# Attention kernel on one core: the high and low parts of the queries are made where they leave PSUM

## What is computed

```python
# layer 0, per token: router over 8 LoRA experts; a_sum = sum of four lora_A products
w = softmax(x @ router_W.T + router_b)
h = nan_to_num(x + SCALING * sum_n w[n] * (a_sum @ lora_B[n].T))       # (4, 512, 1024)
# layer 1: cross attention of 512 tokens on 64 context tokens, 32 heads of 32, then layer norm
Q = (h @ Wq.T + bq); K = (ctx @ Wk.T + bk); V = (ctx @ Wv.T + bv)
attn = softmax(where(mask, Q.K / sqrt(32), -inf))
z = h + (attn @ V) @ Wo.T + bo
out = (z - mean(z)) / sqrt(var(z) + 1e-5) * ln_g + ln_b
```

## Time and profile before

| | |
|---|---|
| median of 3 runs | 742.64 us |
| lowest and highest | 741.37 and 742.81 us |
| span of the profiled execution, first to last instruction | 742.5 us |
| PE busy | 692.8 us (93%) |
| DVE busy | 507.3 us (68%) |
| ACT busy | 322.9 us (43%) |
| POOL busy | 307.7 us (41%) |
| the 16 DMA engines busy | 30.9% |

### The profile page before, as it was taken

How to read it: one execution, slowest core, us unless ns; L and a number is a source line. 1 busy time by engine, 2 the same in 40 slices (tenths; PEclk the granted TensorE clock), 3 DMA queues, 4 the chain that set the end, 5 groups by cost and what they waited for, 6 DMA issues and landing times.

```text
span 742.5 us, 14399 instructions
## 1 busy us (share of the span) xinstructions
PE 692.8 (93%) x4736; PEld 635.2 (86%) x4736; DVE 507.3 (68%) x1169; ACT 322.9 (43%) x1061; POOL 307.7 (41%) x343
## 2 busy tenths in 40 slices
PE   4999999999999999999978869999998999999993
PEld 4896599999999999999978768878887887888883
DVE  1458247465564747364666898999899898998733
ACT  0313211222112212212126997778776778777511
POOL 0111012121121121111233775478767786787644
PEclk9999999999999999999998989999999999999998
DMA  9984121713031311211131363013312232222311
GB/s 284 344 309 163 63 90 38 238 44 128 15 129 41 113 57 54 101 42 71 42 113 58 117 202 95 16 46 123 110 50 86 86 116 85 85 85 72 114 57 57
DMA packets 57012, 76.83 MB, mean 103 GB/s; under 512 B 17025, under 2 KB 38657, under 8 KB 56961
## 3 DMA queue, kind: packets, MB, share of 16 engines
q1 hardware_dynamic: 56960, 76.21, 30.7%
HBM read 48.94 MB, written 27.26 MB: 103 GB/s over the span
## 4 chain that ended last, share of the span: by engine, by line
PE 68%; DVE 17%; issue 6%; ACT 5%; DMA 2%; SPq 1%; POOL 0%; DVEq 0%; ACTq 0%
PE ps L501 18%; PE ps L503 17%; PE ps L502 17%; PE ps L586 4%; PE ps L512 4%; PE ps L599 4%; DVE s_sb L834 2%; DVE p_lo L851 2%; DVE kbd_lo L812 2%; PE ps L531 2%; DVE s_sum L844 1%; PE ps L628 1%; DVE vbd_lo L821 1%; ACT s_sb L1021 1%; DVE act_lo L856 1%
## 5 line engine op out<-in xcount | busy, mean ns | idle before, releaser
L501 PE MATMUL ps<-act_hi,w_hi 128*128 128x256 f32 x512 | 149.1, 291 | 0.6 <-issue 0.6
L503 PE MATMUL ps<-act_hi,w_lo 128*128 128x256 f32 x512 | 145.5, 284 | 0.0
L502 PE MATMUL ps<-act_lo,w_hi 128*128 128x256 f32 x512 | 145.5, 284 | 0.0
L1098 POOL TENSOR_TENSOR h_t<-pos,neg 128x256 f32<-128x256 f32 x64 | 48.2, 753 | 234.1 <-DVE neg L743 234.1
L501 PE MATMUL ps<-w_hi,act_hi 128*128 128x512 f32 x256 | 105.5, 412 | 4.1 <-DVE act_lo L856 4.1
L947 ACT ACTIVATE act_hi<-h_t 128x256 fp32r<-128x256 f32 x64 | 26.7, 418 | 179.5 <-DVE h_t L750 179.5
L503 PE MATMUL ps<-w_hi,act_lo 128*128 128x512 f32 x256 | 100.1, 391 | 0.0
L1021 ACT ACTIVATE s_sb<-s_sb,s_min 128x64 f32<-128x64 f32 x256 | 85.7, 338 | 32.7 <-DVE s_min L839 32.1
L502 PE MATMUL ps<-w_lo,act_hi 128*128 128x512 f32 x256 | 100.0, 390 | 0.0
L501 PEld LDWEIGHTS ps<-act_hi,w_hi 128*128 128x128 f32 x512 | 98.8, 193 | 0.8 <-issue 0.8
L502 PEld LDWEIGHTS ps<-act_lo,w_hi 128*128 128x128 f32 x512 | 98.9, 193 | 0.0
(11 more groups left out here) (102 smaller groups left out, 1721.8 us busy)
## 6 DMA issues: line engine op xcount, KB each, us to landing
x_sb<-xT SPq DMA_DIRECT2D x8, 1024.0 KB, 5.7
h_rows<-hn_sb SPq DMA_DIRECT2D x32, 256.0 KB, 2.2
q_cols<-q_sb SPq DMA_DIRECT2D x32, 256.0 KB, 2.0
q_raw<-q_cols SPq DMA_DIRECT2D x32, 256.0 KB, 3.2
z_sb<-h_rows SPq DMA_DIRECT2D x16, 512.0 KB, 3.7
out<-z_sb SPq DMA_DIRECT2D x16, 512.0 KB, 2.9
wk_raw<-WkT SPq DMA_DIRECT2D x8, 512.0 KB, 7.9
wv_raw<-WvT SPq DMA_DIRECT2D x2, 2048.0 KB, 10.9
```

Of the source, the lines that this page charges most:

```text
L501: pe.matmul(dst, lh, rh, start=(first and j == 0), stop=False)
L502: pe.matmul(dst, lh, rl, start=False, stop=False)
L503: mm = pe.matmul(dst, ll, rh, start=False, stop=(last and j == n - 1))
L1098: pool.tensor_tensor(h_t[m % 4][:], pos[m % 2][:], neg[m % 2][:], ALU.add).then_inc(sign_ready, 1)
```

## The change

ScalarE's `copy_q` now writes the rounded high part to q_sb, and VectorE gets a new `q_low`, which forms the low part from the same PSUM tile, the bias and the high part (one scalar_tensor_tensor). q_copied, on which TensorE waits before it writes that PSUM tile again and SP before it stores, is now signalled by `q_low`; qhi_done comes from `copy_q`. Both parts go to DRAM and back (512 KB a transfer for two chunks), straight into tiles that `scores` reads. `q_high` on ScalarE and the old `q_low` on GpSimd are gone, with q_raw, q_hi and q_lo. `scores` waits for the load itself; `load_q` waits for s_mm, the scores of m-3, as that is what frees its tile. In phase A `q_low` stands in VectorE's program wherever UNIT_A has a "q"; in the first eight steps of phase B it stands behind VectorE's step. The larger q_sb takes 4 KB more of a partition; for it a scratch area that the DMA software keeps in SBUF is made smaller.

```diff
 REGION_3 = max(2 * KC * U + 2 * RC * U + 6 * U + 2 * U // 4, 4 * TU * HPC * V + 8 * U + 8 * U + 4 * U + 2 * KC * V)
-REGION_4 = max(4 * U + 2 * NR * R + KC * LOG + 8 * P * TU + H + NR + TU * (R + 2 * NR + 3) + 64, 2 * H)
+REGION_4 = max(4 * U + 2 * NR * R + KC * LOG + 12 * P * TU + H + NR + TU * (R + 2 * NR + 3) + 64, 2 * H)
...
     hn_d = nc.dram_tensor("h_rows", (NB, UB, U, H), F32, kind="Internal").ap()
-    q_d = nc.dram_tensor("q_cols", (NB, UB, KC // 2, P, 2 * U), F32, kind="Internal").ap()
+    q_d = nc.dram_tensor("q_cols", (NB, UB, KC // 2, P, 4 * U), F32, kind="Internal").ap()
...
         p_lo = [sb(f"p_lo{k}", [P, 2, U], F32R, region3) for k in range(2)]
-        q_hi = [sb(f"q_hi{k}", [P, U], F32R, region3) for k in range(4)]
-        q_lo = [sb(f"q_lo{k}", [P, U], F32R, region3) for k in range(4)]
-        q_raw = [sb(f"q_raw{k}", [P, 2, U], F32, region3) for k in range(2)]
+        q_in_sb = [sb(f"q_in_sb{k}", [P, 2, 2, U], F32R, region3) for k in range(2)]
         k_b = sb("k_b", [P, KC, V], F32, region3)
...
         hn_sb = [sb(f"hn_sb{k}", [P, TU, 2 * P], F32, region4) for k in range(2)]
-        q_sb = [sb(f"q_sb{k}", [P, 2, U], F32, region4) for k in range(2)]
+        q_sb = [sb(f"q_sb{k}", [P, 2, 2, U], F32R, region4) for k in range(2)]
         bo_b = sb("bo_b", [P, H], F32, region4)
...
         hn_stored = [sem(f"hn_stored{k}") for k in range(2)]
-        q_mm, q_copied = sem("q_mm"), sem("q_copied")
+        q_mm, qhi_done, q_copied = sem("q_mm"), sem("qhi_done"), sem("q_copied")
         q_stored = [sem(f"q_stored{k}") for k in range(2)]
...
         q_in = [sem(f"q_in{k}") for k in range(2)]
-        qhi_done, qlo_done = sem("qhi_done"), sem("qlo_done")
         s_mm, s_scaled, min_done = sem("s_mm"), sem("s_scaled"), sem("min_done")
...
                 dst = q_d[i, p, g] if p >= 0 else q_d[i - 1, UB - 1, g]
-                sp.dma_start(dst, q_sb[g % 2][:].rearrange("p a n -> p (a n)")).then_inc(q_stored[g % 2], 16)
+                sp.dma_start(dst, q_sb[g % 2][:].bitcast(F32).rearrange("p l a n -> p (l a n)")).then_inc(q_stored[g % 2], 16)
...
                 p, g = m // KC, (m % KC) // 2
-                wait(sp, qlo_done, i * CB + m - 2)
-                sp.dma_start(q_raw[g % 2][:].rearrange("p a n -> p (a n)"), q_d[i, p, g]).then_inc(q_in[g % 2], 16)
+                wait(sp, s_mm, i * CB + m - 2)
+                sp.dma_start(q_in_sb[g % 2][:].bitcast(F32).rearrange("p l a n -> p (l a n)"), q_d[i, p, g]).then_inc(q_in[g % 2], 16)
...
                 c = m % KC
-                wait(pe, qlo_done, i * CB + m + 1)
+                q_both = q_in_sb[c // 2 % 2]
+                wait(pe, q_in[c // 2 % 2], i * 64 + 16 * (m // 4 + 1))
                 wait(pe, klo_done, 8 * i + 8 * (m // CB) + (8 if c >= 4 else 4))
...
                     mm = three(ps_s[c % 2][:, t * 256:(t + 1) * 256],
-                               [(q_hi[c % 4][:, rows], q_lo[c % 4][:, rows], kbd_hi[:, c, :], kbd_lo[:, c, :])])
+                               [(q_both[:, 0, c % 2, rows], q_both[:, 1, c % 2, rows], kbd_hi[:, c, :], kbd_lo[:, c, :])])
                 mm.then_inc(s_mm, 1)
...
+            def q_low(i, m):
+                c = m % KC
+                wait(dve, qhi_done, i * CB + m + 1)
+                dve.scalar_tensor_tensor(q_sb[c // 2 % 2][:, 1, c % 2, :], ps_q[c % 2], bq_c[:, c:c + 1],
+                                         q_sb[c // 2 % 2][:, 0, c % 2, :], ALU.add, ALU.subtract).then_inc(q_copied, 1)
+
             def update(i, m):
...
             dve.wait_ge(router_in, 32)
-            run_phase_a(dve, {"project": copy_values, "route": router, "expand": u_low, "update": update, "query": lambda i, m: None,
+            run_phase_a(dve, {"project": copy_values, "route": router, "expand": u_low, "update": update, "query": q_low,
                               "flush": flush, "rows": last_h_rows})
...
-            run_phase_b(dve, step, lambda m: None)
+            run_phase_b(dve, step, lambda m: q_low(NB - 1, KC * (UB - 1) + m))
...
                 wait(act, q_stored[c // 2 % 2], i * 64 + 32 * (m // KC) + 16 * (c // 4))
-                act.activation(q_sb[c // 2 % 2][:, c % 2, :], ps_q[c % 2], ACT.Identity, bias=bq_c[:, c:c + 1]).then_inc(q_copied, 1)
+                act.activation(q_sb[c // 2 % 2][:, 0, c % 2, :], ps_q[c % 2], ACT.Identity, bias=bq_c[:, c:c + 1]).then_inc(qhi_done, 1)
...
-            def q_high(i, m):
-                g = m % KC // 2
-                wait(act, q_in[g % 2], i * 64 + 16 * (m // 4 + 1))
-                wait(act, s_mm, i * CB + m - 3)
-                act.activation(q_hi[m % 4][:], q_raw[g % 2][:, m % 2, :], ACT.Copy).then_inc(qhi_done, 1)
-
             def exponential(i, m):
...
                         (k_high if place == "k" else v_high)(i, half)
-                if live(i, m, CB):
-                    q_high(i, m)
                 if live(i, m - 7, CB):
...
-            def q_low(i, m):
-                wait(pool, qhi_done, i * CB + m + 1)
-                pool.tensor_tensor(q_lo[m % 4][:], q_raw[m % KC // 2 % 2][:, m % 2, :], q_hi[m % 4][:],
-                                   ALU.subtract).then_inc(qlo_done, 1)
-
             def normalise_p(i, m):
...
                 p, c = m // KC, m % KC
-                if live(i, m, CB):
-                    q_low(i, m)
                 if live(i, m - 2, CB):
...
     }
-    nc = bacc.Bacc("TRN2", target_bir_lowering=False, num_devices=1)
+    nc = bacc.Bacc("TRN2", target_bir_lowering=False, num_devices=1, dynamic_dma_scratch_size=1024)
     args = [nc.dram_tensor(n, a.shape, mybir.dt.from_np(a.dtype), kind="ExternalInput").ap() for n, a in arrays.items()]
```

## The result

The changed kernel takes 750.67 us in the median of four runs (749.99 to 751.91), the kernel before 742.03 us beside it (741.37 to 742.81): a ratio of 1.0114, 95% interval 1.0095 to 1.0133. The forecast was 745.2 us, with a range up to 749.5. The direction was right, the size was not.

What follows compares the result with a forecast made beforehand. TensorE was taken to bound phase A, TensorE and VectorE in turns phase B. Row copies +4.1, boundary +1.5, opening +1.0, relief -4.0 made +2.6 us on a 742.5 us span: 745.1, stated as 745.2, range 739.8 to 749.5.

Steps and rivals of the forecast that it cites:

- as a load it costs nothing. What counts is the order: Phase A: 64 moved low parts, 22 us of VectorE time, fit its idle time; only what stands behind them matters.
- The row copies, +4.1: Phase A: q_low(0) ahead of the row copies delays TensorE 0.62 us in six units, 0.4 in the seventh; +4.1 us.
- The boundary, +1.5: Between phases A and B: first scores 1.5 us later, from 0.4 delay plus 2.0 larger transfers less 0.9 relief.
- relief of kbd_lo: Boundary: GpSimd's q_low no longer runs beside the four kbd_lo, which take 2.59 us; 0.9 us back.
- The landing of k_b: Boundary: larger query loads and store ahead of k_b hold it up by 1.6 to 2.5 us, taken as 2.0.
- I count no change: Boundary: TensorE's slow clock behind the pause is there before and after, so no cost.
- The opening of phase B, +1.0: First eight steps of phase B: q_low(m) behind ScalarE's copy_q(m) delays VectorE; +1.0 us, between 0 and 2.5.
- The relief, -4.0: Three later batches: without GpSimd's q_low, k and v splits stretch less, 0.4 us in ten splits; -4.0 us.
- Loads hidden: Phase B: doubled loads and stores stay hidden; the next batch's k_b keeps about 4 us of slack.
- The first: Rival, faster: phase B gets down to TensorE's pace, removing all 9.2 us, giving 740.0 us; chance 0.17.
- second: Rival, no change: boundary and opening steps of phase B cost nothing, giving 742.7 us; chance 0.17.
- The third: Rival, much slower: k_b late in three batches, giving 749 us; chance 0.15, including dearer boundary and opening.

Runs made afterwards that it cites:

- a_spread219: Changed kernel with 219 more VectorE instructions, spread over three idle stretches: 744.08 us, ratio 1.0036 to the kernel before.
- e1_rows_first: Changed kernel with VectorE's low part of q0 put behind the three row copies in each unit of phase A: 747.33 us, ratio 1.0067.
- second profile of before: Profile of another run of the unchanged kernel before: span 739.1 us at a time of 740.91 us.
- b_kv_late: Kernel before, with k_b and v_b loads of batches 1 to 3 issued only after scores(13) of the batch before: 743.29 us, ratio 1.0016.
- run 14: Kernel before with 37 more VectorE instructions at its start and k_b and v_b loads released by the scaling of group 13: 747.53 us, one run.
- a_pad256: Changed kernel with 256 more VectorE instructions ahead of the loop, which keeps its place in a 256-instruction block: 760.47 us, ratio 1.0246.
- b_pad37: Kernel before with 37 more VectorE instructions at its start, so the loop stands where the changed kernel has it: 743.89 us, ratio 1.0038.
- a_pad219: Changed kernel with 219 more VectorE instructions, so the loop has the kernel before's place in a 256-instruction block: 749.88 us, ratio 1.0108.
- run 7: Changed kernel with only the high part going through DRAM, 256 KB a transfer, same waits and issue order: 746.35 us, ratio 1.0056.
- b_pad37_kv_later: Same run as run 14: kernel before, 37 more VectorE instructions, k_b and v_b loads released by the scaling of group 13: 747.53 us.
- best_unrolled: Changed kernel with row copies first, k_b and v_b ahead of query loads in every batch, phase B's loop written out: 733.38 us, ratio 0.9878.
- run 12: Same run as a_spread219: changed kernel with 219 more VectorE instructions spread over idle stretches: 744.08 us, ratio 1.0036.
- b_again: Kernel before, unchanged, run and profiled once more: 742.33 us, ratio 0.9998.

## Why the prediction was wrong

**The step that failed** is the sentence on the moved low parts, "as a load it costs nothing. What counts is the order". I counted 64 instructions as VectorE's time and looked for what stands behind each; I didn't count them as length of VectorE's program. They move the loop of phase B by 37 instructions, and in that place VectorE stands still for 5.34 us when it jumps back. Priced by a_spread219 this is 6.6 us of 8.6 us in the medians. In the traces the two steps at the jump are 5.9 us longer than before and 7.3 us longer than in a_spread219, where they have their relief too. Nothing in the trace of before showed it but the 0.47 us at that spot, which I passed over. Without the pause the changed kernel takes 744.08 us, where I had 745.2, with 743.6 to 747.5 as its own range.

**The row copies, +4.1.** Right in place, and near in size: I had 3.7 us for the six units, and their waits grew by 4.1, as q_low takes 484 ns in the middle and not the 433 of its twin. 3.3 us came back in e1_rows_first.

**The boundary, +1.5.** 2.24 measured. The relief of kbd_lo was well sized (2.59 us became 1.76, 0.83 for 0.9). The landing of k_b looks so too (+1.93 for 2.0), but that is luck in part: in the six other profiles with the change's loads and order at the boundary it takes 6.29 to 7.54 us, and with half the traffic still 5.10 for the 4.03 of before, so the volume explains only some of it. The delay ahead of k_b's issue was 1.15 us and not 0.43. The wait for the row copies grew from 1.78 to 2.20 us, about the 0.43 that I had. That leaves 0.7. Behind the wait the granted clock is 0.50 in the window 386 to 388, where before it was 1.00 in 382 to 384, and I had written "I count no change" for the clock; that it makes the 0.7 is likely and not shown by a run of its own.

**The opening of phase B, +1.0.** Not found against the profile shown: 55.45 us from the first scores to batch 1, 56.20 before. Against the second profile of before (54.97) it is +0.5. So q_low(m) costs there less than the 1.2 us by which the two profiles of before differ.

**The relief, -4.0.** 4.45 against the profile shown, 3.47 against the second one of before, where the step of 6.62 us that I read is 5.65. The longest kbd_lo and vbd_lo fell from 854 and 857 ns to 725 and 721: the stretch became less and is not gone. My upper bound was a little high, since 49 x 4.63 is 226.9 and leaves 8.9 us, not 9.2; nothing hangs on it. With the pause gone the step of 6.40 falls to 5.07 as well.

**Loads hidden.** Right: 0.29 us of wait for the keys of batch 3 in a_spread219.

**The rivals.** The first and second didn't come. The third gave 749 and stands nearest in number, but for a wrong reason: it had k_b late in three batches, and what happened is one pause of VectorE in one batch. b_kv_late shows what late keys cost by themselves: 0.16%, 1 us.

**The basis.** The sum began at a span of 742.5 as if it were a median. By chance it is near the median (742.64), so the forecast isn't moved by it: 2.6 us were forecast, 8.6 measured. But the profile is that of a slow execution, with a span 3.4 us longer than the second one, and the comparison of the two traces shows 2 us less than the medians.

**What stays open.** That the pause is VectorE's fetch of its program is not shown by a row that names VectorE. What speaks for it: the place of the loop decides over the pause, in both kernels and both ways; data on the DMA engines lengthen it (2.74 to 4.51 us in run 14); and packets run at that moment on one of the two queues that the page calls "instruction". Its row (packets, MB, share) in the 15 us from 3 us ahead of the jump on, of the changed kernel (606.8 to 621.8), a_pad256 (616.1 to 631.1), b_pad37 (601.8 to 616.8) and the kernel before (605.5 to 620.5), in this order:

```profile
q14 instruction: 4, 0.03, 0.6%
```

```profile
q14 instruction: 4, 0.03, 0.7%
```

```profile
q14 instruction: 7, 0.06, 1.2%
```

```profile
q14 instruction: 3, 0.02, 0.5%
```

In a_spread219 (606.8 to 621.8) and a_pad219 (612.8 to 627.8), which have the change and no pause, there is no such packet. Inside the pause itself there is one with the change and in a_pad256, and two in b_pad37. So both kernels have four packets more around the jump where it is dear. Over a whole execution the count tells less: it is 28 and 27 in two profiles of the kernel before, 32 in b_pad37, 24 in a_pad219, 28 in a_pad256, but only 26 in the changed kernel, in which the programs of other engines are different too. The rows don't say which engine a packet is for, so this is strong support, and not proof. Where between 780 and 817 the edge lies wasn't tried, nor whether the loops of the other engines have such places. Nor is it clear where all that half the traffic gives comes from (run 7).

## What to carry to other kernels

Instructions added to an engine also lengthen its program: where a loop follows, look in the trace at its jump back for a gap that ends in "issue", and if there is one, write the loop out or move it by a few instructions in idle time before anything else is judged (here 6.6 us, three quarters of the whole loss). In a list of work in fixed order, put a new instruction behind those that another engine is waiting for: 0.48 us of VectorE in front of the row copies cost 3.3 us in seven places. Where a phase begins with several loads, try first the one whose data pass through most steps before the first matmul: k_b, which has to be split, ahead of the queries, the row copies mended and the loop moved turned together the change from 1.1% slower into 1.2% faster.

## What the hardware showed

- The same loop, with the same instructions, costs 0.43 to 0.47 us at its jump back in one place of VectorE's program and 2.74 to 5.52 us in another (b_pad37, the changed kernel, e1_rows_first, a_pad256), and 256 instructions more bring the pause back to 5.07. With idle DMA engines it was 2.74; where data flowed on, it ended about 3 us behind them (615.09 for 612.0 with the change, 610.38 for 607.6 in b_pad37_kv_later). In the place without a pause the same loads cost the jump nothing (0.43 us in a_spread219).
- Around a dear jump back four packets more run on a queue of kind "instruction" than around a cheap one (7 for 3 in the kernel before, 4 for none in the changed one).
- A wait that is already met is not free on VectorE: 97 ns for an instruction with two of them (13.93 us for 144, 16.36 us for 169). The 65 ns that I named ahead of run 12 were too low.
- After a wait of 1.62 us the granted clock stayed at 1.00 (best_unrolled, 392 to 398); after 4.71 us it was 0.59 (the changed kernel, 398 to 404), and the first step took 5.67 us, not 3.68. In between, after waits of 2.68 us (b_again) and 3.28 us (a_spread219), it was 0.72 in the six us from the first scores on, and the first step took 5.15 us.
